# Keys split into bf16 parts in PSUM by ScalarE casts and TensorE subtractions, a half batch per head pair, in place of GpSimd's splits in SBUF

## What is computed

```python
x = x + self_attention(layernorm(x))     # 16 heads of 64, fixed point: every product is truncated to 1/4096
x = x + cross_attention(layernorm(x), ctx)  # ctx (4, 1601, 128) is both keys and values, 16 heads of 8
x = x + mixture_of_experts(layernorm(x))

def cross_attention(q, ctx):
    scores = einsum('bhqd,bhkd->bhqk', split_heads(q), split_heads(ctx)) + mask
    ctx_ = einsum('bhqk,bhkd->bhqd', softmax(scores), split_heads(ctx))
    return relu(ctx_ @ wo_w.T + wo_b)
```

## Time and profile before

| | |
|---|---|
| median of 3 runs | 750.12 us (749.71 to 751.29) |
| the profiled execution, its own time | 743.64 us |
| its span in the trace | 741.9 us |
| mean granted TensorE clock | 0.906 of full speed |
| busy: PE, DVE, ACT, POOL | 585.1, 531.5, 445.2, 185.7 us |
| self-attention, first `weights_T` of head pair 0 to the end of head pair 6 | 32.2 to 231.2 us |

### The profile page before, as it was taken

One profiled execution on the slowest core, in us unless ns is written; L12 is line 12 of the kernel. 1 busy time (PEld: TensorE's weight loads), 2 busy tenths in 40 slices (PEclk: granted clock), 3 DMA queues, 4 the chain that ended last, 5 costly groups with the idle time before them and its releaser, 6 DMA issues.

```text
span 741.9 us, 13437 instructions
## 1 busy us (share of the span) xinstructions
PE 585.1 (79%) x4759; PEld 289.4 (39%) x4759; DVE 531.5 (72%) x896; ACT 445.2 (60%) x818; POOL 185.7 (25%) x234
## 2 busy tenths in 40 slices
PE   3775548888896856899999988889886875999981
PEld 2453335555554743333333333333331232444441
DVE  4466698899889987688888888788783245555541
ACT  3553338888889412687867876778674752334330
POOL 4325570000011233332115101500040044122222
PEclk9876679999999985999999999999996795999996
DMA  8332364724576802601090109000029001011103
GB/s 209 97 121 92 100 219 175 199 60 122 143 158 131 151 1 89 227 3 47 2 222 24 47 2 211 35 3 1 2 79 319 2 28 51 22 33 34 33 21 93
DMA packets 32667, 66.91 MB, mean 90 GB/s; under 512 B 4542, under 2 KB 21322, under 8 KB 32164
## 3 DMA queue, kind: packets, MB, share of 16 engines
q0 software_dynamic: 8960, 45.07, 22.9%
q1 hardware_dynamic: 22068, 20.31, 9.1%
q10 hardware_dynamic: 1584, 0.79, 0.4%
HBM read 46.45 MB, written 19.30 MB: 89 GB/s over the span
## 4 chain that ended last, share of the span: by engine, by line
PE 43%; DVE 32%; ACT 9%; issue 8%; DMA 5%; SPq 1%; DVEq 0%; ACTq 0%; POOLq 0%; POOL 0%
DVE smax L1647 12%; PE pair L1079 10%; DVE region_p L1550 6%; PE pair L1054 6%; PE pair L1233 5%; PE pair L1009 4%; PE pair L910 3%; PE pair L874 3%; DVE region_p L1520 3%; ACT region_p L1410 2%; ACT region_p L1329 2%; DVE region_p L1823 2%; PE pair L896 2%; DVE region_p L1553 2%; PE pair L963 1%
## 5 line engine op out<-in xcount | busy, mean ns | idle before, releaser
L1647 DVE TENSOR_REDUCE smax<-pair 128x2 f32<-128x1024 f32 x192 | 225.5, 1218 | 55.7 <-PE pair L1009 55.0
L1410 ACT ACTIVATE region_p<-pair 128x1024 f32<-128x1024 f32 (+3 forms) x277 | 217.5, 812 | 68.3 <-PE pair L1054 63.1
L910 PE MATMUL pair<-ident,region_p 128*128 128x128 f32 x256 | 39.3, 302 | 45.3 <-DVE region_p L1553 45.3
L1520 DVE SCALAR_TENSOR_TENSOR region_p<-region_p 128x1024 int16<-128x1024 int16 (+1 forms) x56 | 67.6, 1229 | 9.1 <-ACT region_p L1315 6.6
L1079 PE MATMUL pair<-region_p 128*32 128x256 f32 (+1 forms) x832 | 69.8, 410 | 0.5 <-ACT region_p L1417 0.4
L1079 PE MATMUL pair<-region_p,region_b 128*32 128x256 f32 (+1 forms) x832 | 66.5, 391 | 0.4 <-ACT region_p L1417 0.4
L1550 DVE TENSOR_SCALAR region_p<-region_p,rnorm 128x256 f32<-128x256 f32 x128 | 62.1, 548 | 1.1
L1054 PE MATMUL pair<-region_b,region_k 59*128 59x256 bf16 (+1 forms) x416 | 54.7, 273 | 8.2 <-ACT region_p L1410 4.0
L1009 PE MATMUL pair<-region_k,region_b 56*128 56x512 bf16 (+1 forms) x256 | 44.5, 365 | 16.8 <-DVE smax L1647 15.6
L910 PEld LDWEIGHTS pair<-ident,region_p 128*128 128x128 f32 x256 | 31.0, 154 | 59.9 <-DVE region_p L1553 59.2
L1329 ACT ACTIVATE region_p<-region_p 128x256 f32<-128x256 int16 x128 | 51.3, 409 | 0.0
(11 more groups left out here) (244 smaller groups left out, 968.3 us busy)
## 6 DMA issues: line engine op xcount, KB each, us to landing
kimg<-region_k SPq DMA_DIRECT2D x56, 200.1 KB
region_k<-kimg POOLq DMA_DIRECT2D x8, 1400.9 KB, 12.4
region_b<-in_mask_Bx1xSxS_ff POOLq DMA_DIRECT2D x12, 800.5 KB, 7.0
region_p<-in_mask_Bx1xSxS_ff POOLq DMA_DIRECT2D x4, 800.5 KB, 13.2
region_b<-in_ctx SPq DMA_DIRECT2D x4, 768.0 KB
region_k<-in_L_ffn_W POOLq DMA_DIRECT2D x3, 1024.0 KB, 8.4
xdisp<-region_x POOLq DMA_DIRECT2D x1, 2322.0 KB, 21.1
xdisp<-region_x POOLq DMA_DIRECT2D x1, 2257.5 KB, 18.4
```

What stands on the lines that cost most here:

```text
L910: last = pe.transpose(pair[1][:, c:c + 128], attn[:, b % 2, a:a + 128], ident[:, :])
L1410: act.activation(pT[0:rows, first // 3 % 2, k:k + size], home[0:rows, 0:size], ACT.Exp).then_inc(expt_made, 1)
L1520: return dve.scalar_tensor_tensor(out_, floor16, 0.0, floor16, ALU.is_lt, ALU.add)
L1647: last = dve.tensor_reduce(units[:, :, c // 3, c % 3], both, AX.X, ALU.max)
```

## The change

1. The four batches of ctx become eight halves (1024 and 577 columns). `half_of(h)` gives the batch, the columns and the PSUM home. `ctx_transposes(h)` puts a half there, and it stays there.
2. `ctx_cast(h, i)` on ACT casts the PSUM half to bf16 part i in SBUF. `ctx_subtract(h, i)` on PE multiplies that part by `negb`, the identity times minus one in bf16, and accumulates the product in the same PSUM columns, which leaves the rest. Three casts and two subtractions make a half. The tensor `ctxT`, `ctx_move` and POOL's `split` are gone.
3. Halves 0 and 1 are made in the start, between the projections of head pair 0. Half hp + 2 is made in head pair hp (0 to 5), at b = 2 and b = 3.
4. PE's and ACT's head pairs are written out eight times; DVE keeps its loop.
5. In the start, ACT takes the standard deviation of the layer norm first, before it moves the projection weights. wo is transposed and moved later. V of head pair 0 has another PSUM home.
6. All four batches of ctx are loaded in the start, behind the small inputs. The image stores now stand in SP's queue between pairs of weight loads, and `ones_load` is done in two places. The pads stores go to the end of head pairs 1 and 2, the keys of batch 0 to head pairs 3 and 4, the keys of batch 1 behind `mask_load(0)`. The probes of the mask use the other slot, and the values of batch 0 are moved by POOL in the start.

```diff
+            def ctx_transposes(h):
+                k, _, _, home = half_of(h)
+                pe.wait_ge(ctx_loaded[k], 32)
+                if h == 1:
+                    pe.wait_ge(cast_made, 3)
+                elif h:
+                    pe.wait_ge(qkv_rounded, 3 * (h - 1) + 3)
...
+            def ctx_subtract(h, i):
+
+                k, first, size, home = half_of(h)
+                if h == 0:
+                    pe.wait_ge(ident_made, 3)
+                pe.wait_ge(cast_made, 3 * h + i + 1)
+                for c in range(0, size, 512):
+                    end = min(c + 512, size)
+                    last = pe.matmul(home[:, c:end], negb, kparts[:, k % 2, i, first + c:first + end],
+                                     start=False, stop=True, skip_group_check=True)
+                last.then_inc(ctx_sub, 1)
...
+            def ctx_cast(h, i):
+
+                k, first, size, home = half_of(h)
+                if i == 0:
+                    act.wait_ge(ctx_T, h + 1)
+                    if k >= 2 and h % 2 == 0:
+                        act.wait_ge(kimg_written[k % 2], 224)
+                else:
+                    act.wait_ge(ctx_sub, 2 * h + i)
+                act.activation(kparts[:, k % 2, i, first:first + size], home[:, 0:size], ACT.Copy).then_inc(cast_made, 1)
...
             def head_pair(hp):
-                first, last = (isinstance(hp, int) and hp == end for end in (0, HP - 1))
+                first, last = hp == 0, hp == HP - 1
+                half = hp + 2 if hp + 2 < 2 * B else None
                 for b in range(B):
                     if b == 0 and not last:
                         weights_move(hp + 1)
                     exps(hp, b)
                     if b or not first:
                         attn_move(*batch_of(hp, b, -1))
+                    if half is not None and b == 3:
+                        ctx_cast(half, 1)
                     if b == 2 and not last:
                         round_qkv(hp + 1, 2)
                     if b + 2 < B or not last:
                         round_dots(*batch_of(hp, b, 2))
                     if b < 2 and not last:
                         round_qkv(hp + 1, b)
-                    if first and b:
-                        ctx_move(b, (2, 2))
+                    if half is not None and b >= 2:
+                        ctx_cast(half, 0 if b == 2 else 2)
...
-            for k in range(2, 4):
-                sp.wait_ge(ctx_T, 2 * (k - 1))
-                ctx_load(sp, CTX_ORDER[k], ctx_home[k], ctx_loaded[k % 2])
-                if k == 2:
-                    weights_load(1)
-                    image_store(0)
-            weights_load(2)
-            image_store(1)
...
+            weights_load(1)
+            image_store(0)
+            sp.wait_ge(ones_made, 1)
+            ones_load(0)
+            for k in range(1, B):
+                weights_load(2 * k)
+                weights_load(2 * k + 1)
+                image_store(k)
```

More of the change, by code:

```diff
@@ L369, in qkv_home @@
         def qkv_home(hp, c):
-            return pair[(2, 0, 1)[c]] if isinstance(hp, int) and hp == 0 else pair[2]
+            return pair[(2, 0, 2)[c]] if hp == 0 else pair[2]
         kimg = nc.dram_tensor("kimg", (B, 128, HP, S2), BF16, kind="Internal").ap()
@@ L705, in _ @@
             mask_load(0)
+            for k in range(2):
+                pool.wait_ge(kimg_written[k], 448)
+            for a in range(2):
+                keys_load(1, a)
             pool.dma_start(xdisp[:, D + 1:ROW].rearrange("(n p) c -> p (n c)", p=128), pad_index.bitcast(F32),
@@ L943, in head_pair @@
                         dots(*batch_of(hp, b, 2))
+                    if half is not None and b == 2:
+                        ctx_transposes(half)
+                    if half is not None and b == 3:
+                        ctx_subtract(half, 0)
                     if b < 2 and not last:
@@ L947, in head_pair @@
                         attn_values(*batch_of(hp, b, -1))
+                    if half is not None and b == 3:
+                        ctx_subtract(half, 1)
                     if last and b == B - 1:
@@ L965, in project_out @@
                 last.then_inc(proj_mm, 1)
-            repeat(pe, HP, head_pair)
+            for hp in range(HP):
+                head_pair(hp)
             attn_values(HP - 1, B - 1)
@@ L1339, in mask_probe @@
             def mask_probe(u, slot):
-                act.wait_ge(probe_loaded[slot], 16 * (u + 1) if slot == 0 else 16)
-                column = mask_hi[:, u:u + 1] if isinstance(u, int) else mask_hi[:, bass.ds(u, 1)]
-                act.activation(mask_sb[:, slot, :], mask_sb[:, slot, :], ACT.Abs, accum_out=column).then_inc(probe_made, 1)
-            weights_move(0)
-            for c in range(3):
-                round_qkv(0, c)
+                act.wait_ge(probe_loaded[slot], 16 * (u + 1) if slot else 16)
+                act.activation(mask_sb[:, slot, :], mask_sb[:, slot, :], ACT.Abs,
+                               accum_out=mask_hi[:, u:u + 1]).then_inc(probe_made, 1)
+            std_of(1)
+            act.wait_ge(wproj_T, 1)
+            act.activation(wpT[:, :, :].rearrange("p h d -> p (h d)"), pair[3][:, :], ACT.Copy).then_inc(wpT_made, 1)
+            ctx_cast(0, 0)
+            xn_move(1, xnT[:, :], pair[2][:, :])
+            weights_move(0)
+            ctx_cast(0, 1)
+            round_qkv(0, 0)
+            ctx_cast(0, 2)
+            round_qkv(0, 1)
+            ctx_cast(1, 0)
+            round_qkv(0, 2)
+            ctx_cast(1, 1)
             round_dots(0, 0)
+            ctx_cast(1, 2)
             round_dots(0, 1)
+            act.wait_ge(small_T, 1)
+            act.activation(woT[:, :], pair[3][:, 512:640], ACT.Copy).then_inc(smallT_made, 1)
             def head_pair(hp):
-                first, last = (isinstance(hp, int) and hp == end for end in (0, HP - 1))
+                first, last = hp == 0, hp == HP - 1
+                half = hp + 2 if hp + 2 < 2 * B else None
                 for b in range(B):
```

160 lines of the change are left out of this document (72 added, 88 removed).

## The result

| | before | after |
|---|---|---|
| median of timed executions (4 and 4) | 750.70 us (749.71 to 751.67) | 739.93 us (738.72 to 741.03) |
| profiled execution, its span | 743.64, 741.9 us | 739.85, 738.1 us |
| granted clock, mean | 0.906 | 0.911 |

The ratio is 0.986, with a 95% interval of 0.984 to 0.988: 10.8 us faster. The forecast was 713 us, with a range of 704 to 730, so 27 us of the gain are missing.

A forecast was written before the change was run, and what follows sets the result against it. The prediction took POOL's split, which blocks DVE's divisions in head pairs 0 and 1, as the bound. 743.64 - 33.9 (self-attention) - 3.0 (start) = 706.7 us, with 6.5 us for the median 713 us; range 704 to 730.

The forecast's parts named there:

- I count 0: Image stores and weight loads in SP's queue: weights land 21.2 us after a store starts, just in time; no cost.
- late weights: Rival: weights behind stores come late, 18 us stall ahead of head pair 3, 10 ahead of 5; about 764 us; chance 0.04.
- strict turns: Rival: each cast waits for its subtraction and attention work waits behind both; 23 us more, 736 us; chance 0.08.
- The prediction's own case: Whole kernel: the forecast of 713 us, with 707 to 718 us as its own range; chance 0.52.
- What held the kernel: Head pairs 0 and 1: POOL's split blocks DVE's divisions and small scalings; 25.8 us of DVE time lost.
- Head pair 0: Self-attention's first head pair: 22.1 us steady, 4.5 for filling the pipeline, 0.5 for later exponentials; 27.1 us against 55.7.
- the rival in which more comes back: Rival: head pair 0's filling of 4.5 us shrinks and the casts disappear in waits; 703 us; chance 0.12.
- Head pairs 1 to 5: ACT's idle time absorbs 1.0 us of casts per half; 1.7 us stay for a long half, 0.6 for a short.
- Both rivals on the casts: Rivals: casts cost in full, nothing absorbed, 726 us, chance 0.24; or strict turns, 736 us, chance 0.08.
- The start: Before head pair 0: the earlier root starts its chain 5.1 us earlier, against added casts; a gain of 3 us taken.
- The loop written out: PE's and ACT's head pairs without a loop: nothing counted, in either direction.
- The median above the profile: Whole kernel: the median of timed runs stood 6.5 us above the profiled execution, and this was added to 706.7 us.

The follow-up runs named there:

- late-root kernel: The kernel with the weights on ACT's queue, with ACT moving the projection weights before it takes the layer norm's root, as before: 713.46 us, ratio 0.960.

## Why the prediction was wrong

**The step that failed** is "I count 0", under stores and loads. The sum there, 15.4 + 5.8 = 21.2 us against 23.8, takes the store's duration from a row beside which POOL's queue moved nothing, and the landing of the weights from a median. It finds a margin of 2.6 us at most and leaves out what the change itself puts beside the store: the pads in head pair 2, the keys in 4. Measured were 16.3 + 29.7 = 46.0 us ahead of head pair 3 and 16.3 + 13.1 = 29.4 ahead of 5, so it is mostly the landing that was mis-sized. The runs put 28.1 us of waiting in the place of the 0.

The rival *late weights* named the place and the partners: 18 us ahead of head pair 3 (22.05 measured) and 10 ahead of 5 (6.04), 28 together. That the total agrees is partly luck, since one part is 4 us too low and the other 4 too high. It got a chance of 0.04 because I let it count only together with the strict turns, which would have made the kernel slower. The prediction's own case with its stall added, 713 + 28 = 741 us, is the measured time within 1.2 us, but no such case had a chance in it. (Luck has a part here too: without the stall self-attention gained 39.2 us where I had 36.9, and the later stages lost 7.4 where I had added 6.5.)

The argument against the rival was that the engines share out their time. They do share between queues. But inside SP's queue the weights stand behind the rest of 14 stores, which themselves have the smaller share: over the 29.7 us q0 moves 3.88 MB in 55.7% of the engines' time and q1 1.97 MB in 20.2%. Of these 1.97 MB the weights are 0.19, so by an estimate from this row about nine of the 14 stores were still to land when the weights were asked for.

The Trainium skill ("DMA: Bandwidth & Descriptors", "Queues, rings and completion order") says both halves of this: an engine takes turns between the queues that have work for it, a packet at a time, and within a queue it takes descriptors in the order of its ring. By that rule a small load on a queue of its own should come through a full machine quickly, and behind a store it should not. The two runs agree: 11.0 us at most on ACT's queue, in the head pair with a DMA share of 0.78, and 29.7 us behind the store.

**What held the kernel.** Right. The division is back at 1.14 us for four:

```profile
31.14 1.14 DVE L1588 TENSOR_SCALAR region_p<-region_p,rnorm 128x256 f32<-128x256 f32 x4
...
50.20 1.14 DVE L1588 TENSOR_SCALAR region_p<-region_p,rnorm 128x256 f32<-128x256 f32 x4
```

Taking the split away from before gave 29.7 us. Of these DVE's busy time makes 24.6; the forecast had 25.8 for DVE. The rest came with it in the same run, at a clock of 0.92 and 1.00 instead of 0.69 and 0.84; no run takes these two apart.

**Head pair 0.** The forecast of 27.1 was met (27.08), and the filling is as I kept it: from the first weight transposes to the end of the attention transposes of batch 1 pass 16.2 us (25.97 to 42.20), with 16.1 in before. But this rests on the clock of the one execution: it was low from 32 to 41 us, as in before's filling. Six kernels with the full casts took 24.12 to 27.08 us for head pair 0, by their mean clock: 1.00 (24.12), 0.93 (25.71, 25.77, 25.77) and 0.87 (26.97, 27.08). At a clock of 1.00 the filling and the context transposes make 1.2 us without the casts (23.28 against 22.1), where I had 4.5 for the filling. So the rival in which more comes back was right on this term in one of the six. In all six PE is busy for 3.6 of the first 6.0 to 6.4 us of the head pair and waits 2.9 us for DVE ahead of its first attention transposes; why the clock falls behind that in five of them and not in the sixth is open.

**Head pairs 1 to 5.** Without the stalls 22.06, 23.57, 23.65, 22.94 and 24.63 us, forecast 22.7, 23.8, 22.7, 23.8 and 22.7. The long one of head pair 5 has a clock of 0.88 behind the second stall. In the kernel with the weights on ACT's queue head pairs 0 to 5 sum up to 142.4 where the forecast has 142.8. That a short half costs less than a long one did not show: with no stall around, 3 costs 1.7 and 4 costs 0.7. I had read the waits right: ACT's wait for weight transposes is 0.2 us in all in that kernel over head pairs 1 to 5, 3.6 in the one without casts and 3.6 in before. The casts fill it. Both rivals on the casts fall: they had 15.3 and 29.1 us for the casts of six head pairs, and 5.6 were measured, 8.4 with the clock of head pair 0.

**The start.** 6.2 us are gained (25.97 against 32.21), forecast 3.0. The early root makes 3.0 of them. The other 3.2 are there with the late root too: its first weight transposes of all come at 15.82 us, those of before at 19.15. Before's rows, then DVE's in the late-root kernel:

```profile
13.18 3.44 DVE L1515 TENSOR_SCALAR region_x<-x_in,meanvar,rstd 128x128 f32<-128x128 f32 x8
...
14.96 1.58 POOL L638 CAST region_k<-region_k 128x1601 bf16<-128x1601 f32 x1 [9.75 <-ACT region_k L1288]
...
16.68 1.09 PE L846 MATMUL pair<-ident,region_x 128*128 128x128 f32 x8 [2.54 <-DVE region_x L1515]
...
19.15 0.88 PE L861 MATMUL pair<-ident,wnat 128*128 128x128 f32 x3 [1.26 <-ACT woT L1303]
```

```profile
11.87 2.14 DVE L1552 TENSOR_SCALAR region_x<-x_in,meanvar,rstd 128x128 f32<-128x128 f32 x8
```

The split costs here as well, which I had overlooked: DVE's normalisation takes 3.44 us beside its first cast and 2.14 without it (2.18 in before without the split), and PE waits for it. Another 1.3 us are that the root comes at 11.39 instead of 12.70, since the projection weights landed later in this execution of before (8.38 against 7.08, and 7.03 in before with its loops written out). The last 0.7 fit PE's wait for the move of wo, which the change puts later. No run isolated these three.

**The loop written out.** Inside the loops next to nothing, as forecast (22.02 against 22.10 us for a head pair). The run as a whole is 0.6% slower than before, with 0.2 to 0.9% as its interval, which neither the forecast nor its rival had, and which lies in stages that the edit doesn't touch.

**The median above the profile.** The 6.5 us that I added stand between before's profiled execution and its median. Most of them are likely the experts' stage. SP's queue of before, then of after, first and last of the rows of this stage:

```profile
619.23 87.01 SPq L613 DMA_DIRECT2D region_p<-xdisp  x23
728.50 0.95 SPq L515 DMA_DIRECT2D region_p<-ydisp  x2
```

```profile
609.88 92.60 SPq L620 DMA_DIRECT2D region_p<-xdisp  x23
724.72 0.95 SPq L528 DMA_DIRECT2D region_p<-ydisp  x2
```

That is 109.3 us in before's profiled execution and 114.8 in after's. In every other profile here it is 114.7 to 115.0, that of before with its loops written out among them, so it isn't the change. With it the sum closes. From 743.64 take the 11.1 us by which head pair 7 starts earlier (220.1 against 231.2), add 5.6 for the experts and 1.8 for what lies between: 739.9 us, and 739.85 was the profiled execution. What makes the stage long or short is open, and so is the 1.8.

## What to carry to other kernels

When a change moves a transfer, draw up for each queue what stands behind it and, for each stretch, what the other queues put on the DMA engines at the same time. A load that is "just in time" by durations taken on quiet engines can be late on full ones, and a rival whose mechanism costs 28 us needs a chance of its own, not only one in company of others. A small load that feeds the next stage belongs on a queue without big stores ahead of it, or the big transfers of other queues belong in the stretches without such a store; either cure took the waits away here (to 0 and to 0.56 us), and moving the pads to the end of the stage did not make the kernel faster. A difference between two traces that goes with the clock should be looked up in its place in time before it is put down to an edit: here the low clock had ended 6 us before the work that one would blame for it.

## What the runs showed of the hardware

In the kernel after, a load of 192 KB landed in 2.5 us at best and in 29.7 us at worst, from the same line; only what was ahead of it and beside it differed. On ACT's queue, with the DMA engines 0.78 busy, 11.0 us was the most. In the rows that show one image store by itself, SP needed 10.9 to 15.7 us to issue its 14 transfers with no large store or load of keys of POOL's beside it, and 14.3 to 16.3 with one: the ranges overlap, and the stall is mostly in the landing. Eight small instructions of DVE in the start took 3.44 us beside a cast on POOL and 2.14 without it. The same work in head pair 0 took 24.12 to 27.08 us in six kernels, with a mean granted clock of 1.00 to 0.87; where there is a low stretch, it lies between 32 and 44 us. And a stage that no edit touches took 109.3 us in one profiled execution and 114.7 to 115.0 in nine others, 5.4 to 5.7 us apart, which is half of the change's measured gain; a sum made against one profiled execution should check that stage first.
